# Second attention, second routing and second experts in one block, with the tokens, the first preparation and the position softmax laid out anew

## The chip, the cores and the metric

The kernel runs on one core of one Trainium2 chip. The metric is the device time of one execution in microseconds (us). The core has five engines that run their own instruction streams and meet at semaphores: PE (TensorE, matrix products), DVE (VectorE), ACT (ScalarE), POOL (GpSimd) and SP (SyncE, which here issues transfers). SBUF is the on-chip memory of 128 partitions, PSUM the eight banks into which PE writes.

## What is computed

The reference is an audio tower of two layers on 16 signals of 4096 samples. Cut to what matters:

```python
h = tok(x)          # cubic interpolation by 4, 255 windows of 64, 0.5*(x+1.3)^2 + 0.5*exp(-0.5*(x-0.7)^2),
                    # |FFT|, sigmoid mask against 0.12 of the row's maximum, soft minimum with 0.9 of it
h = h + attn0(layernorm(h))      # 8 heads, rank 32, values projected to 64 per head
h = h + ffn0(layernorm(h))       # 16 experts, top 2, relu, own layer norm behind it
h = h + attn1(layernorm(h))      # 8 heads of 8; (1-g)*softmax(q k) + g*softmax(position score)
h = h + moe(layernorm(h))        # 8 experts, top 2, gelu: out = tokens + sum_e combine_e * (h_e @ w2_e + b2_e)
```

A position score is `wpos0 * d + wpos2 * d*d + bias` with d the distance of two windows; its softmax over the windows doesn't depend on the signals. The 16 x 255 tokens of 64 numbers stand as 32 tiles of 128 x 64 (the last row of each second tile is padding).

## The kernel before, in words

The program is eight phases, one after the other, each a block of instruction streams with a barrier of all engines behind it (L161): `tokens`, `attention_prep0`, `attention0`, `experts0`, `attention_prep1`, `attention1`, `experts_prep1`, `experts1`. Inside a phase the order on each engine is written out by hand and the waits are semaphores; an engine that waits holds all that stands behind it in its stream. `link` (class `Chain`) makes an engine wait for its own last instruction.

*tokens.* SP and ACT issue the signal loads: 127 partitions of 16 runs of 20 samples from each queue (L222, L242), then single partitions, taps, constants and raw weights. `interpolate` (L209 to L216) multiplies and adds five taps; DVE does tile 0 (1024 elements a partition) and six batches of tile 1, POOL the other ten. ACT makes two squares and an exponential of each tile (L251 to L254), DVE sums them (L293) and splits the weights into three bf16 parts (L298 to L302); PE turns and transforms four groups (L361, L368), and ACT and DVE do the spectrum (L306 to L325). POOL then works out the position scores of eight heads (L345 to L347).

*attention_prep0.* Norm on DVE (L430 to L445), which writes each tile twice; PE turns it (L387), and `ColumnParts` splits the turned columns into three bf16 parts: ACT (L392, L398), DVE (L406, L408), POOL (L412).

*attention0.* 16 batches, two slots each. PE makes projections, scores (L636), turnings (L646) and outputs (L663); ACT the exponentials (L734), the copies of projections (L726) and of outputs (L742, once a batch). In the first four slots ACT also makes the exponentials of the position scores (L773) and DVE their maxima (`pos_max`, L848).

*experts0.* 8 chunks of 512 tokens, each 8 steps of two experts. PE: `hidden` (L1629), `second` (L1637), and for the next chunk columns (L1603), logits (L1611) and the turning of the combined weights (L1619). DVE: weighting (L1848), summing (L1828) and, as `extra` of each step, the routing of the next chunk (L1752 to L1785) and two norms. ACT: relu (L1720) and scalings. POOL: inverse roots (L531 to L540) and a copy a chunk (L1879). SP spreads the weights over partitions through DRAM (L1925).

*attention_prep1* makes values and position values and zeroes the padding on POOL.

*attention1.* 16 batches of four units (scores for the maximum, L1278 and L1431; turned scores, L1284; exponentials, L1399; outputs, L1294). A batch's tail (blend L1469, projection L1333, addition L1474, norm L518 to L543) runs up to three batches behind, so after the last unit there are eleven slots of tails alone.

*experts_prep1.* PE turns the tiles (L947) and multiplies by the router (L956); DVE takes the best two (L995 to L1002), and `combine` (L1013 to L1028) makes the weights of half the tiles at a time, in three bf16 parts; PE turns them (L964) and ACT copies them out (L977). POOL zeroes `ct` (L1042) and `selb`.

*experts1.* 8 chunks of two groups: PE `hidden` (L1070), `spread` of the weights (L1078), `second` (L1087) with three products for the output biases (L1091) and the turning of the sum (L1099); ACT gelu (L1138) and `y_out` (L1128); DVE weighting (L1169) and `finish` (L1157, L1158); SP stores each chunk with two transfers, of 128 and of 127 partitions (L1185). The lines of the biases are:

```python
for n in range(3):
    last = nc.tensor.matmul(Y[0:D], b2p[:, n], ct[:, c], start=False, stop=False)
```

## Time and profile before

| | us |
|---|---|
| median of 3 runs (909.3 to 911.83) | 911.78 |
| the profiled execution's own time | 908.39 |
| its span, first to last instruction | 906.5 |
| PE busy | 686.8 (76%) |
| DVE busy | 642.9 (71%) |
| ACT busy | 490.5 (54%) |
| POOL busy | 342.4 (38%) |

The phases end, by the timeline, near 98 (tokens), 126 (first preparation), 377 (first attention), 574 (first experts), 607 (second preparation), 805 (second attention), 840 (preparation of the second experts) and 906 us (second experts). A row of the timeline gives start, duration, engine, line, operation and tiles; "x4" means four merged into one row. PE's clock stands in the windows as a share of 2.4 GHz: 1.00, or 0.50 for 1.2 GHz.

### The profile page before, as it was taken

To read this page: it belongs to the slowest core of one execution; us is meant where nothing else is said; L and a number is where in the kernel's file an instruction comes from. 1 tells how busy PE (TensorE), PEld (TensorE's weight loads), DVE (VectorE), ACT (ScalarE), POOL (GpSimd) and SP (SyncE) were. 2 spreads that over 40 slices of the span, in tenths; PEclk is the share of its full clock that TensorE was granted. 3 is DMA by queue.
4 is the path that set the end of the run, shared out by engine and by line. 5 is a ranking of instruction groups with operands and counts; after the bars stand their busy time and mean duration, and the time that the engine had idled before them with its cause. 6 is when DMAs were issued, how large, how long until landed. Compare 5 with 4: busy or idle time off the path is not lost. (4 is left out here: it accounts for less than half of the span.)

```text
span 906.5 us, 16572 instructions
## 1 busy us (share of the span) xinstructions
PE 686.8 (76%) x5035; PEld 375.4 (41%) x5035; DVE 642.9 (71%) x1681; ACT 490.5 (54%) x1237; POOL 342.4 (38%) x374
## 2 busy tenths in 40 slices
PE   0003146899999999579999996568999999966995
PEld 0002124566666666323333322444555555556332
DVE  0299856988889889357788886746788888836343
ACT  0035446877677766245666664525666666622532
POOL 0299343577686776511122112442232222230000
PEclk9997557999999999889999998777999999965898
DMA  0200200000000000132323331000000000000000
GB/s 9 82 0 0 92 1 0 2 1 0 0 0 1 0 0 1 69 95 95 97 95 107 108 110 52 1 2 1 2 1 0 0 0 0 0 1 0 7 21 20
DMA packets 21241, 24.31 MB, mean 27 GB/s; under 512 B 11854, under 2 KB 12110, under 8 KB 20942
## 3 DMA queue, kind: packets, MB, share of 16 engines
q1 hardware_dynamic: 18989, 23.31, 8.3%
q10 hardware_dynamic: 2209, 0.49, 0.3%
q8 instruction: 19, 0.31, 0.1%
q14 instruction: 24, 0.20, 0.1%
HBM read 22.48 MB, written 1.31 MB: 26 GB/s over the span
## 5 line engine op out<-in xcount | busy, mean ns | idle before, releaser
L883 POOL TENSOR_TENSOR big<-big 128x1024 f32<-128x1024 f32 x64 | 120.4, 1893 | 80.7 <-DVE big L805 80.7
L734 ACT ACTIVATE big<-ps,big 128x255 f32<-128x255 f32 x256 | 117.5, 486 | 10.0 <-DVE big L799 9.5
L1720 ACT ACTIVATE big<-ps,b1s 128x512 f32<-128x512 f32 x128 | 80.5, 681 | 40.9 <-PE ps L1629 40.8
L799 DVE TENSOR_REDUCE big<-ps 128x4 f32<-128x1020 f32 x64 | 74.6, 1205 | 27.6 <-PE ps L636 27.6
L1431 DVE TENSOR_REDUCE big<-ps 128x4 f32<-128x1020 f32 x65 | 79.2, 1218 | 16.3 <-PE ps L1278 14.4
L812 DVE COPY mid<-ps 128x512 f32<-128x512 f32 x128 | 82.0, 681 | 5.7 <-DVE res L817 2.9
L1637 PE MATMUL ps<-big,w2s 128*64 128x512 f32 x256 | 69.0, 618 | 7.9 <-ACT big L1720 7.9
L1629 PE MATMUL ps<-big,wall 64*128 64x512 f32 x256 | 74.5, 650 | 0.0
L726 ACT ACTIVATE big<-ps 128x512 f32<-128x512 f32 x64 | 39.4, 616 | 64.0 <-PE ps L624 38.5
L646 PE MATMUL ps<-cst,big 128*128 128x128 f32 x512 | 71.1, 278 | 3.8 <-DVE mid L812 2.2
L1848 DVE SCALAR_TENSOR_TENSOR big<-ps,b2s,mid 128x512 f32<-128x512 f32 x64 | 48.0, 750 | 31.9 <-issue 12.0
L663 PE MATMUL ps<-mid,big 128*64 128x256 f32 (+1 forms) x512 | 69.5, 392 | 0.3 <-DVE mid L812 0.3
L1399 ACT ACTIVATE big<-ps 128x1024 f32<-128x1024 f32 x64 | 65.9, 1029 | 0.3
L646 PEld LDWEIGHTS ps<-cst,big 128*128 128x128 f32 x512 | 57.1, 141 | 20.8 <-DVE mid L812 7.8
L536 POOL TENSOR_TENSOR big<-big 128x4 f32<-128x4 f32 x16 | 16.1, 1009 | 120.6 <-DVE big L526 120.6
L1272 PE MATMUL ps<-big,selqk 128*128 128x256 bf16 x396 | 57.1, 283 | 3.5 <-POOL big L1509 2.4
L1369 ACT ACTIVATE big<-ps 128x256 bf16<-128x256 f32 x66 | 25.7, 389 | 61.4 <-PE ps L1272 61.3
L734 ACT ACTIVATION_READ_ACCUMULATOR big<-ps,big 128x1 f32 x256 | 56.3, 220 | 0.0
L361 PE MATMUL ps<-cst,big 128*128 128x128 f32 x16 | 3.6, 384 | 66.4 <-DVE big L293 66.4
L387 PE MATMUL ps<-cst,big 128*128 128x128 f32 x64 | 14.5, 373 | 49.7 <-DVE big L445 32.8
L636 PE MATMUL ps<-big 32*128 32x256 f32 x512 | 38.5, 417 | 8.2 <-ACT big L734 7.9
L1272 PEld LDWEIGHTS ps<-big,selqk 128*128 128x128 bf16 x396 | 34.3, 100 | 22.1 <-issue 13.9
(254 smaller groups left out, 1448.8 us busy)
## 6 DMA issues: line engine op xcount, KB each, us to landing
mid<-spread_w SPq DMA_DIRECT2D x128, 128.0 KB, 2.8
mid<-in_split_sel SPq DMA_DIRECT2D x1, 1536.0 KB, 6.2
wall<-in_w SPq DMA_DIRECT2D x1, 1280.0 KB, 7.1
cst<-in_consts SPq DMA_DIRECT2D x1, 666.5 KB, 5.0
mid<-in_w_raw SPq DMA_DIRECT2D x1, 620.0 KB, 6.3
w2s<-in_w SPq DMA_DIRECT2D x1, 512.0 KB, 3.2
out_tokens<-res SPq DMA_DIRECT2D x8, 64.0 KB
out_tokens<-res SPq DMA_DIRECT2D x8, 63.5 KB
```

Source lines behind the costliest of these rows:

```text
L646: last = nc.tensor.transpose(AT[:, j, c, P * tq:P * tq + P], e_sb[r % 4][:, j, tq, P * c:P * c + P], ident)
L663: last = nc.tensor.matmul(O[D * j:D * j + D, par], val[par][0:n, c, D * h:D * h + D], a_sb[r % 4][0:n, j, c], start=(g == 0 and a == 0 and ...
L734: last = nc.scalar.activation(e_sb[r % 4][:, jj, tq, 0:NW], S[:, 2 * (r % 2) + jj, tq, 0:NW], ACT.Exp, scale=-1.0, bias=minus[r % 4][:, jj ...
L799: nc.vector.tensor_reduce(minus[r % 4], S[:, 2 * a:2 * a + 2, :, 0:NW], AX.X, ALU.min).then_inc(s_mx, 1)
L812: nc.vector.tensor_copy(a_sb[r % 4][:, j], AT[:, j]).then_inc(s_at, 1)
L883: nc.gpsimd.tensor_tensor(e_sb[r % 4], e_sb[r % 4], bc(inverse[r % 4].unsqueeze(3), [P, 2, 2, 256]), ALU.mult).then_inc(s_A, 1)
L1272: last = nc.tensor.matmul(out_, selqk[:, 2 * p + n, part], parts[par][:, part], start=(part == 0), stop=(part == 2))
L1399: nc.scalar.activation(e_sb[(k - 1) % 4], T, ACT.Exp, scale=scale).then_inc(s_E, 1)
L1431: nc.vector.tensor_reduce(mx[k % 2], S[:, :, :, 0:NW], AX.X, ALU.max).then_inc(s_max, 1)
L1629: last = nc.tensor.matmul(H1(e, j), wst[0][half, f:f + P], xc[q][half], start=True, stop=True)
L1637: last = nc.tensor.matmul(Y(e)[D * j:D * j + D], w2s[0][:, 2 * e + j], hid[e % 2][j], start=True, stop=True)
L1720: last = nc.scalar.activation(hid[e % 2][j], H1(e, j), ACT.Relu, bias=b1s[0][:, 2 * e + j:2 * e + j + 1])
```

## The change

Seven parts:

1. The signal loads are cut into 112 and 15 partitions, and the taps go first on ACT's queue. DVE interpolates everything, in three stages (tile 0; two halves of tile 1), between which the weight splitting and the sums stand; ACT copies the weight parts; PSUM banks are no longer shared between groups. The absolute value moves from ACT to DVE, and products with broadcast maxima are joined with the sums.
2. The position scores leave `tokens` for POOL in `experts0`; maxima and exponentials leave `attention0` for DVE and ACT in `experts0`, one head a chunk.
3. `attention_prep0` splits the normed rows into bf16 parts before they are turned (`RowParts`), in place of the columns after.
4. The output biases of the second experts become one product of 96 rows: the combined weights are laid out three times (`c3`, with zeroed padding), the biases in three parts below each other.
5. `experts_prep1` and `experts1` move into the block of `attention1`. The turning, logits and routing stand between the tails of the last batches on PE, ACT and DVE.
6. `combine` and the turned weights come in two halves: `combine(1)` between the first and second chunk of the experts, the last four `weights` in chunk 2.
7. Each chunk is stored with four transfers, of 112 and 16 and of 112 and 15 partitions.

```diff
+                    sp.dma_start(sig[1:113, 0], windows(1, 112)).then_inc(s_sig[0], 16)
+                    sp.dma_start(sig[113:P, 0], windows(113, P - 113)).then_inc(s_sig[0], 16)
+                    sp.dma_start(sig[0:1, 0, :, 2:REACH], bass.AP(tensor=x.tensor, offset=0, ap=[[SIG, 1], [SIG, B], [1, REACH - 2]])).then_inc(s_sig[0], 16)
+                    sp.dma_start(raw, w_raw).then_inc(s_raw, 16)
+                    sp.dma_start(cst[:], consts).then_inc(s_cst, 16)
                     sp.dma_start(posw[:], pos_in).then_inc(s_pw_in, 16)
...
                     act.dma_start(tw, taps).then_inc(s_tw, 16)
+                    act.dma_start(sig[0:112, 1], windows(P, 112)).then_inc(s_sig[1], 16)
+                    act.dma_start(sig[112:P - 1, 1], windows(P + 112, P - 113)).then_inc(s_sig[1], 16)
+                    act.dma_start(sig[P - 1:P, 1], windows(NW - 1, 1)).then_inc(s_sig[1], 16)
...
+                    dve.wait_ge(s_sig[0], 16 * 3)
+                    dve.wait_ge(s_tw, 16)
                     link(nc.vector.tensor_copy(sig[0:1, 0, :, 0:2], bc(sig[0:1, 0, :, 2:3], [1, B, 2])))
-                    interpolate(nc.vector, link, 0, 0, B).then_inc(s_z[0], 1)
-                    interpolate(nc.vector, link, 1, B - 6, 6).then_inc(s_z2, 1)
-                    for t in (0, 1):
-                        dve.wait_ge(s_sq, 3 * t + 3)
-                        nc.vector.scalar_tensor_tensor(out=z[:, t].rearrange("p b j -> p (b j)"), in0=gauss[:, t].rearrange("p b j -> p (b j)"), scalar=0.5,
-                                                       in1=poly[:, t].rearrange("p b j -> p (b j)"), op0=ALU.mult, op1=ALU.add).then_inc(s_kw, 1)
-                    dve.wait_ge(s_raw, 16)
-                    hi, md, lo = (w64[:, s] for s in range(3))
-                    link(nc.vector.tensor_copy(hi, raw))
-                    link(nc.vector.tensor_tensor(raw_rest, raw, hi, ALU.subtract))
-                    link(nc.vector.tensor_copy(md, raw_rest))
+                    for k in (1, 2, 3, 4, 0):
+                        tap(*STAGES[0], k)
+                    dve.wait_ge(s_sig[1], 16 * 3)
+                    for k in (1, 2):
+                        tap(*STAGES[1], k)
+                    dve.wait_ge(s_hi, 1)
+                    nc.vector.tensor_tensor(raw_rest, raw, hi, ALU.subtract).then_inc(s_rest, 1)
+                    kernelled(0)
+                    for k in (3, 4, 0):
+                        tap(*STAGES[1], k)
...
-                    pool.wait_ge(s_sig, 16 * 4)
-                    interpolate(nc.gpsimd, link, 1, 0, B - 6).then_inc(s_z[1], 1)
...
+            def high(self, act, c, tiles):
+                nc.scalar.activation(self.ra[:, c, :, 0], tiles, ACT.Copy).then_inc(self.s_hi, 1)
+                nc.scalar.activation(self.rb[:, c, :, 0], tiles, ACT.Copy).then_inc(self.s_h2, 1)
+            def subtract(self, dve, c, tiles):
+                dve.wait_ge(self.s_hi, c + 1)
+                nc.vector.tensor_tensor(self.rest[:, c], tiles, self.ra[:, c, :, 0], ALU.subtract).then_inc(self.s_rest, 1)
+            def middle(self, act, c):
+                act.wait_ge(self.s_rest, c + 1)
+                nc.scalar.activation(self.ra[:, c, :, 1], self.rest[:, c], ACT.Copy).then_inc(self.s_md, 1)
+            def low(self, pool, c):
+                pool.wait_ge(self.s_md, c + 1)
+                nc.gpsimd.tensor_tensor(self.rb[:, c, :, 1], self.rest[:, c], self.ra[:, c, :, 1], ALU.subtract).then_inc(self.s_lo, 1)
+            def turn(self, pe, c):
+                pe.wait_ge(self.s_lo, c + 1)
+                pe.wait_ge(self.s_h2, c + 1)
+                if c >= self.RING:
+                    pe.wait_ge(self.s_col, 2 * (c - self.RING) + 2)
+                for k, rows in enumerate((self.ra, self.rb)):
+                    for t in range(TC):
+                        last = nc.tensor.transpose(self.turned[:, c % self.RING, k, P * t:P * t + P],
+                                                   rows[:, c, t].rearrange("p a d -> p (a d)"), ident_b[:])
+                last.then_inc(self.s_tr, 1)
+            def columns_out(self, dve, c):
+                dve.wait_ge(self.s_tr, c + 1)
+                for k in range(2):
+                    nc.vector.tensor_copy(columns[k][:, c], self.turned[:, c % self.RING, k]).then_inc(self.s_col, 1)
         def attention_prep0():
             sq = mid[:, 0:2048].rearrange("p (t d) -> p t d", t=NT)
...
+                    for c in range(CH + 3):
+                        if c < CH:
+                            normed(c)
+                        if 1 <= c <= CH:
+                            rows.subtract(dve, c - 1, xr[:, c - 1])
+                        if c >= 3:
+                            rows.columns_out(dve, c - 3)
...
-                        if known and j == 0:
-                            for h in (2 * k, 2 * k + 1):
-                                act.wait_ge(s_pmax, h + 1)
-                                for tq in range(2):
-                                    nc.scalar.activation(pexp[:, tq, h], pexp[:, tq, h], ACT.Exp, bias=pmax[:, tq, h:h + 1],
-                                                         accum_out=psum[:, tq, h:h + 1]).then_inc(s_pexp, 1)
...
+            c3 = mid[:, 3072:3072 + NT * 48].bitcast(BF16).rearrange("p (t r s) -> p t r s", t=NT, r=3)
...
+                    x_turn(0)
+                    x_turn(1)
+                    slot(B // 2, 2, ("tail",))
+                    logits(0)
+                    x_turn(2)
+                    slot(B // 2, 3, ("tail",))
+                    logits(1)
+                    x_turn(3)
+                    logits(2)
+                    x_turn(4)
+                    logits(3)
+                    x_turn(5)
+                    slot(B // 2, 6, ("tail",))
+                    logits(4)
+                    slot(B // 2, 7, ("tail",))
+                    x_turn(6)
+                    logits(5)
+                    x_turn(7)
+                    logits(6)
+                    logits(7)
+                    hidden(0, 0)
+                    pe.wait_ge(s_O, QUADS * B)
+                    pe.wait_ge(s_fin, B)
+                    for d in range(4):
+                        weights(d)
+                    for c in range(CH):
+                        hidden(c, 1)
+                        spread(c, 0)
+                        if c >= 1:
+                            second(c - 1, 1)
+                        if c == 2:
+                            pe.wait_ge(s_wgt, GROUPS * c + 1)
+                            for d in range(4, CH):
+                                weights(d)
+                        if c < CH - 1:
+                            hidden(c + 1, 0)
+                        spread(c, 1)
+                        if c >= 1:
+                            sum_turn(c - 1)
+                        second(c, 0)
+                    second(CH - 1, 1)
+                    sum_turn(CH - 1)
...
+                    columns_out(0)
+                    slot(B // 2, 2, ("o",))
+                    for c in range(1, 6):
+                        columns_out(c)
+                    slot(B // 2, 6, ())
+                    gap(0)
+                    for c in range(6, CH):
+                        columns_out(c)
+                    for d in range(4):
+                        weights(d)
+                    gap(1)
+                    for c in range(CH):
+                        for g in range(GROUPS):
+                            s = GROUPS * c + g
+                            act.wait_ge(s_h, s + 1)
+                            if s >= 2:
+                                act.wait_ge(s_wgt, s - 1)
+                            for n in range(2):
+                                last = nc.scalar.activation(hid[2 * g + n], H1(g, n), ACT.Gelu, bias=b1s[1][:, 2 * g + n:2 * g + n + 1])
+                            last.then_inc(s_hid, 1)
+                            if g == 0 and c >= 1:
+                                y_out(c - 1)
+                            if g == 0 and c == 2:
+                                for d in range(4, CH):
+                                    weights(d)
+                    y_out(CH - 1)
 
                 @block.vector
                 def _(dve):
...
+                        thrice = lambda a: bc(a[:, tl].unsqueeze(2), [P, half, 3, E])
+                        hi, md, lo = (c3[:, tl, :, E * n:E * n + E] for n in range(3))
+                        if n == 0:
+                            dve.wait_ge(s_pad3, 1)
+                        link(nc.vector.tensor_copy(hi, thrice(comb)))
+                        link(nc.vector.tensor_tensor(pick[:, tl], comb[:, tl], hi[:, :, 0], ALU.subtract))
+                        link(nc.vector.tensor_copy(md, thrice(pick)))
+                        nc.vector.tensor_tensor(lo, thrice(pick), md, ALU.subtract).then_inc(s_c3, 1)
...
+                    slot(B // 2, 1, ())
+                    best(0)
+                    slot(B // 2, 2, ())
+                    best(1)
+                    slot(B // 2, 3, ())
+                    best(2)
+                    slot(B // 2, 5, ())
+                    best(3)
+                    difference(0)
+                    slot(B // 2, 6, ())
+                    slot(B // 2, 7, ())
+                    slot(B // 2 + 1, 1, ())
+                    combine(0)
+                    slot(B // 2 + 1, 2, ())
+                    for c in range(4, CH):
+                        best(c)
+                    difference(1)
+                    for c in range(CH):
+                        weigh(c, 0)
+                        weigh(c, 1)
+                        if c == 0:
+                            combine(1)
+                        else:
+                            finish(c - 1)
+                    finish(CH - 1)
...
+                    nc.gpsimd.memset(c3, 0.0).then_inc(s_pad3, 1)
...
+                            for first, n in ((0, 112), (112, 16 - tq)):
+                                src = res[first:first + n].rearrange("p (b t) d -> p b t d", t=2)
+                                sp.dma_start(out[bass.ds(2 * c, 2), P * tq + first:P * tq + first + n].rearrange("b w d -> w b d"),
+                                             src[:, bass.ds(2 * c, 2), tq]).then_inc(s_out, 16)
...
-                            for n in range(3):
-                                last = nc.tensor.matmul(Y[0:D], b2p[:, n], ct[:, c], start=False, stop=False)
...
+                            last = nc.tensor.matmul(Y1[0:D], b2p[:], ct[0:96, c], start=False, stop=False)
...
+                        act.wait_ge(s_pmax, h + 1)
+                        for tq in range(2):
+                            nc.scalar.activation(pexp[:, tq, h], pexp[:, tq, h], ACT.Exp, bias=pmax[:, tq, h:h + 1],
+                                                 accum_out=psum[:, tq, h:h + 1]).then_inc(s_pexp, 1)
...
+                            if e == COLUMNS + 1:
+                                pos_exps(c)
...
+                    def pos_max(h):
+                        dve.wait_ge(s_pos, h + 1)
+                        link(nc.vector.tensor_reduce(pmax[:, :, h], pexp[:, :, h, 0:NW], AX.X, ALU.max))
+                        nc.vector.tensor_scalar(pmax[:, :, h], pmax[:, :, h], -1.0, None, ALU.mult).then_inc(s_pmax, 1)
...
-                        extra = [[first], [total, stats], [variance, second], [places], [shares, spread], [next_stats, next_variance], [gain, shift], [add]]
+                        extra = [[first], [total, stats], [variance, second], [places, lambda: pos_max(c)], [shares, spread], [next_stats, next_variance], [gain, shift], [add]]
...
+                    def pos_scores(h):
+                        link_p(nc.gpsimd.tensor_scalar(term, dist, posw[:, 0, h:h + 1], zb[:, h:h + 1], ALU.mult, ALU.add))
+                        link_p(nc.gpsimd.tensor_scalar(pexp[:, :, h], d2, posw[:, 2, h:h + 1], 0.0, ALU.mult, ALU.add))
+                        link_p(nc.gpsimd.tensor_tensor(pexp[:, :, h], pexp[:, :, h], term, ALU.add))
+                        nc.gpsimd.memset(pexp[:, :, h, NW:NW + 1], -1e30).then_inc(s_pos, 1)
...
+                        for h in ((0, 1), (2,), (3,), (4,), (5,), (6,), (7,), ())[c]:
+                            pos_scores(h)
...
-        phase(attention1)
-        phase(experts_prep1)
-        phase(experts1)
+        phase(attention1_and_experts1)
```

## Rows read from the trace of the kernel before

**Rows 1.** Windows of 50 us: stretch, length, busy time of each engine (instructions), PE clock, DMA share, GB/s.
```profile
450.00:500.00 50.00, 47.14 (x213) 15.55 (x211) 42.40 (x145) 33.88 (x65) 11.01 (x18) 1.00 0.31 98
```

**Rows 2.** Finer windows, same columns: the first load, and the last stores.
```profile
10.00:14.00 4.00, 0.00 (x0) 0.00 (x0) 0.00 (x0) 0.00 (x0) 0.00 (x0) 1.00 0.09 10
...
900.00:901.00 1.00, 0.00 (x0) 0.00 (x0) 0.00 (x0) 0.00 (x0) 0.00 (x0) 0.50 0.35 80
901.00:902.00 1.00, 0.00 (x0) 0.00 (x0) 0.00 (x0) 0.00 (x0) 0.00 (x0) 0.50 0.08 18
```

**Rows 3.** Timeline of the tokens: start us, us, engine, line, operation, out<-in, shape, [idle before].
```profile
1.15 30.85 SPq L225 DMA_DIRECT2D mid<-in_x  x1
...
40.10 1.23 DVE L209 TENSOR_TENSOR big<-mid 128x1024 f32<-128x1024 f32 x1 [4.27 <-DMA mid<-in_taps]
...
41.36 2.25 DVE L211 TENSOR_TENSOR mid<-mid 128x1024 f32<-128x1024 f32 x1
...
59.28 0.56 DVE L211 TENSOR_TENSOR mid<-mid 128x384 f32<-128x384 f32 x1
...
78.50 2.70 DVE L306 TENSOR_TENSOR big<-big 128x496 f32<-128x496 f32 x2
...
97.29 0.68 DVE L325 TENSOR_TENSOR res<-big 128x496 f32<-128x496 f32 x1
```

**Rows 4.** Timeline of the first preparation, and one row of the second attention.
```profile
110.36 0.69 DVE L406 TENSOR_TENSOR big<-ps,cols_area 64x512 f32<-64x512 f32 x1 [0.70 <-ACT cols_area L392]
...
124.68 1.15 POOL L412 TENSOR_TENSOR cols_area<-big,cols_area 64x512 bf16<-64x512 f32 x1 [0.34 <-ACT cols_area L398]
...
790.04 0.29 DVE L1453 TENSOR_TENSOR big<-big,ps 128x256 bf16<-128x256 bf16 x1
```

**Rows 5.** Timeline of ScalarE in the first attention: position exponentials, copies of the outputs.
```profile
152.37 0.56 ACT L773 ACTIVATE pexp<-pexp,pmax 128x256 f32<-128x256 f32 x1
...
152.86 0.55 ACT L773 ACTIVATE pexp<-pexp,pmax 128x256 f32<-128x256 f32 x1
...
166.68 0.39 ACT L742 ACTIVATE big<-ps 128x256 f32<-128x256 f32 x1
...
182.43 0.40 ACT L742 ACTIVATE big<-ps 128x256 f32<-128x256 f32 x1
...
196.47 0.39 ACT L742 ACTIVATE big<-ps 128x256 f32<-128x256 f32 x1
```

**Rows 6.** A maximum of positions; waits in the first experts: engine line <- for, us, times, longest.
```profile
127.77 0.67 DVE L848 TENSOR_REDUCE pmax<-pexp 128x2 f32<-128x510 f32 x1
...
PE ps L1637 <- ACT big L1720: 7.6, 8, 1.1
...
PE ps L1619 <- DVE big L1785: 2.1, 7, 0.9
```

**Rows 7.** Timeline of POOL: a zeroing of bf16.
```profile
805.91 3.51 POOL L1042 MEMSET big<- 128x4096 bf16 x1 [1.76 <-POOLq L161]
```

**Rows 8.** Timeline of the last three phases, and one logit product and one chain row.
```profile
795.74 1.07 PE L1294 MATMUL ps<-big,mid 128*32 128x256 f32 x16 [1.12 <-ACT big L1399]
...
804.19 0.60 DVE L543 TENSOR_SCALAR big<-res,big 128x128 f32<-128x128 f32 x2 [0.81 <-POOL big L531]
...
812.48 1.87 PE L956 MATMUL ps<-gates,big 64*128 64x8 f32 x8
...
829.74 0.62 DVE L1013 TENSOR_TENSOR big<-cst,big 128x128 f32<-128x128 f32 x2
...
845.08 1.28 DVE L1169 TENSOR_TENSOR big<-big,ps 128x512 f32<-128x512 f32 x2 [8.47 <-PE ps L1078]
...
898.21 0.43 DVE L1158 TENSOR_TENSOR res<-res,big 128x256 f32<-128x256 f32 x1
...
396.04 0.95 PE L1611 MATMUL ps<-gates,big 64*128 64x16 f32 x7
...
854.72 0.64 PE ps L1091 x3
```

680 lines of the change are left out of this document (310 added, 370 removed).

## Prediction

> **What bounds the kernel now.** I read the table of windows first, then the timeline of the stretches it made doubtful, then the waits. There is no one bound: the kernel is eight phases in a row, and each has its own. The first experts are held by TensorE (PE), 47.1 of 50 us busy at full clock, with VectorE (DVE) close behind at 42.4 [rows 1]. The start is held by a transfer: the small load of L225 sits 30.85 us in its queue, and the first interpolation operation starts at 40.10 us [rows 3]. Meanwhile the 16 DMA engines are 9% busy, about 1.5 of them, at 10 GB/s [rows 2]. Then DVE and GpSimd (POOL) take turns: a 128x1024 DVE operation takes 1.23 us when POOL comes second and 2.25 us right after; one of 384 elements with POOL out of the way takes 0.56 [rows 3]. The tokens end at 97.97 us. After the second attention comes a stretch in which nothing is full: the last normalised tile is written at 804.79, the first weighting of the second experts starts at 845.08 [rows 8]. From there PE is gapless.
>
> **Working, part by part.** The sum is made against the profiled execution: span 906.5 us, its own time 908.39; the median of the three runs is 911.78, so 3.4 above it.
>
> *Signal loads.* Each load of 127 partitions becomes one of 112 and one of 15, the taps go first on their queue and the constants come behind. The row shows two loads of 2032 pieces of 80 bytes at 10 GB/s: 325 KB in 31 us [rows 2]. A store of 128 rows beside one of 127 shows the other speed: 80 GB/s in its microsecond, against 18 GB/s for the 127-row one alone [rows 2]. That is some 240 pieces of 256 bytes in 1 us. At that pace 2032 pieces take about 8 us, at a sixteenth of the present time 2 us; with 2 us until the first byte moves and 1 to 2 us to land the first operation starts between 5 and 14 us. I take 8.5, nearer the low end, since that microsecond was not full. Gain 31.6, bounds 26 to 35. (The Trainium skill, DMA: Bandwidth & Descriptors, section on why a DMA increments its semaphore by 16, says that the number of engines is the largest k up to 16 that divides the outermost dimension: 127 gives 1, 112 gives 16, 15 gives 15. The 9% agrees; by it alone the operation would start at about 6.)
>
> *Interpolation on DVE alone.* Tile 0: seven operations of 1024 at 1.26 and two of 256 at about 0.45, 9.7 us. Tile 1 in two halves of 512: 5.7 each. Laid out with what stands between them on DVE (weight remainders 1.3 twice, sums of window parts 1.2 and 0.65), the last tap ends 25.7 us after the start. Then ScalarE (ACT) window parts 1.9, sum 0.6, and the last two groups through PE and ACT, 4.3: 32.5. The spectrum takes 19.5 us today from the power sums [rows 3], with POOL in the way; without it and with three fewer small operations I work out 14. Together 46.5, plus 1 for three POOL operations left in the stage: 47.5 against 57.9 today (40.10 to 97.97). Gain 10.4, bounds 7 to 13. (The Trainium skill, SBUF — State Buffer, section on two separate sides, calls this an exclusive lock, held for the whole instruction, between a DVE operation with two SBUF inputs and a POOL operation that reads SBUF; the alternation agrees.)
>
> *First preparation.* From the reciprocals on it takes 18 us today, to 125.83, at about 2.2 us of DVE a chunk (0.69 for the remainder [rows 4]). The new order is 0.42 + 0.42 and two copies of 512 bf16 out of PSUM. A bf16 addition out of PSUM of 256 takes 0.29 [rows 4], so 0.42 each, at worst 0.69. That is 1.7 to 2.2 us a chunk, with POOL's remainder in turns with it. Gain 1, bounds -3 to +3.
>
> *Position softmax.* It leaves POOL's part of the tokens (in the way, counted above) and ACT in the first attention: 16 exponentials, 0.49 us from one to the next [rows 5], 7.8 in all. The output copies stand 15.75 us apart with it and 14.04 after [rows 5], which is 0.85 a slot at least, four slots. Gain 5, bounds 3.4 to 7.8. It arrives in the first experts. There POOL's four instructions a head (about 2.5 us) have room. ACT's two exponentials fall where it has half a microsecond of slack and PE has none to lose before its next activation: about 0. DVE's maximum (0.67) and the negation behind it cost 0.90 a head [rows 6] and stand right ahead of the combining of weights. PE turns these weights and waits for them already today, 7 times, 2.1 us in all [rows 6]; it has no slack to give back. So 7 chunks by 0.9, 6.3. Turns with POOL in the same stretch: between 0 and 2 us a chunk, I take 0.4, as the maximum itself covers most of POOL's work. Loss 9, bounds 0 to 19.
>
> *Zeroing of the padded weights.* 3072 bf16 on POOL, ahead of the fetch for which the second attention's first projection waits; 4096 took 3.51 [rows 7]. Loss 2.6.
>
> *One block.* Its start is the end of the last full unit, 794.2. The first two turnings follow the last outputs at 796.8. With PE at work its clock stays at 2.4 GHz, where 7 small logit products take 0.95; at the present 1.2 GHz 8 take 1.87 [rows 8]. DVE then sets the pace: best(0) from 799.5, four routings of 1.3 with the remaining norms between them to 809.3, the last addition and its norm to 810.5, combine(0) 4.5 (3.45 for one today, and three of its operations grow threefold, 0.3 each) to 815, scale, four more routings to 821. Then weights out 2.4, a table load of 1.3 and the activation: first weighting at 826.3. PE idles 6 us before x_turn(7). If it falls to 1.2 GHz there and stays, 2 to 4 later; if the logits run at 1.2 GHz throughout, 832.8. Today 845.08: gain 18.8, bounds 12 to 20. The new waits on DVE hold back the last norms, behind them the last x_turn; that is in the sum.
>
> *Second experts.* 53.6 us from first weighting to last addition. Biases as one product: three take 0.64 in the chain [rows 8], so 0.43 a chunk, 3.4. Against it combine(1), 4.4 us on DVE where 2.05 were idle: 2.4; and the late weights in chunk 2, PE 1.5 and a late activation: 2.3. Net loss 1.3, bounds -1 to +4. Queue at the end: last addition at 898.64, span 906.5. The 127-row store runs until about 905 at 18 GB/s [rows 2]; now four issues and spread rows: gain 2.5, bounds 1 to 4.
>
> **Sum.** -31.6 - 10.4 - 1 - 5 + 9 + 2.6 - 18.8 + 1.3 - 2.5 = -56.4: 852.0 on the profiled execution's scale. The median of the runs stood 3.4 above the profiled execution and its lowest 0.9; I put 853.
>
> **Rivals.** (a) *The move into the first experts is hidden*: the stall of PE on its activations (7.6 us in 8 times [rows 6]) would absorb it. Against it: the weights are awaited behind that stall. Then 845. (b) *The move costs double*: POOL and DVE take turns for all of POOL's 2.5 us in the critical stretch, 0.9 + 1.8 by 7 chunks, 19 instead of 9: 863. For it: the 2.25 us row. Against: POOL begins while DVE reads PSUM. (c) *Small pieces are paced by how fast they are described, not by the engines*: at the 7.7 ns of today (31.3 us by 4064) 4064 pieces take 31 us in any split. With both halves in flight the first is done near 20 and the operation starts at 22: 867. Against it: the 80 GB/s row, less than 4 ns a piece. (d) *The routing in between pays little*: DVE waits at best(0) and best(1) while PE waits for DVE, clock at 1.2 GHz: first weighting past 835, 862. (e) *Slower*: DVE becomes the bound of the first experts because each of its two-input operations waits for POOL. It decides once a chunk grows from 21.05 to above 29.5 us (the 57 us and the 9 already counted, over 8 chunks); POOL's whole new work is 2.5 a chunk and ACT's 1, so it would have to be paid three times: 915. (f) *The loads do not spread at all*: start at 40 as now, 885.
>
> **Chances.** Forecast 0.55; (a) 0.16; (b) 0.11; (c) 0.07; (d) 0.07; (e) 0.01; (f) 0.03. The parts' own bounds, taken together, give about 10 either way; (a), (b) and (d) are inside 839 to 868 and (c) is at its edge, so this is the range. Measurements tell 0.3% apart, 2.7 us: faster 0.98, same 0.01, slower 0.01.
>
> **What would show it.** First interpolation operation at 6 to 10 us, and several DMA engines at once before it; 1024-element operations all near 1.25; tokens' end at 54 to 58. Output copies of the first attention 14.0 apart from the first on. Chunks of the first experts at 22.0 to 22.5 instead of 21.05, with PE waiting for the combined weights. First weighting of the second experts 32 us after the last full unit (today 51), chunks of 6.26 instead of 6.69, two of them longer. The prediction is wrong if the first operation starts past 15, if a chunk of the first experts passes 24, or if PE is at 1.2 GHz through the routing.

## The result, and the profile after the change

The changed kernel takes 870.63 us (median of 4 runs, 863.96 to 872.24) beside 911.45 for the kernel before (4 runs, 909.3 to 911.83): ratio 0.9548, 95% interval 0.9502 to 0.9595. The forecast was 853.0 with a range of 839 to 868. So the direction was right, and the gain is 41 us where 59 had been forecast. The profiled execution took 863.96 us with a span of 861.9. Against the forecast on the profiled scale, 852.0, that is 12 us too slow. The other 5.7 us lie between the profiled execution and the median: they are 6.7 us apart, where the forecast had put 1.0 (852.0 to 853). The profiled execution was the fastest of the four.

The page of the changed kernel, span, busy times and two of the slice rows:

```profile
span 861.9 us, 16537 instructions
...
PE 690.9 (80%) x5051; PEld 373.7 (43%) x5051; DVE 628.8 (73%) x1699; ACT 491.0 (57%) x1249; POOL 308.6 (36%) x372
...
PE   0404699999999983988889884566999999998897
...
PEclk9955599999999995999998998776999999995899
```

Look at the clock row, a slice of which is 21.5 us: the twenty-second (452 to 474 us) is an 8, in the middle of the first experts, which ran at full clock in all their chunks before the change. Slices this long hide the other, shorter falls.

The span falls apart into ten stretches. Each border is one instruction found in both timelines, and the forecast column is the prediction's own term:

| stretch, to | before | after | change | forecast |
|---|---|---|---|---|
| first interpolation operation starts | 40.10 | 6.98 | -33.1 | -31.6 |
| tokens' last operation ends | 57.87 | 48.94 | -8.9 | -10.4 |
| first attention's first fetch (POOL) | 28.71 | 26.41 | -2.3 | -1 |
| first experts' first fetch (POOL) | 252.6 | 247.3 | -5.3 | -5 |
| second preparation's first operation (POOL) | 195.2 | 214.8 | **+19.6** | +9 |
| second attention's first maximum (DVE) starts | 42.2 | 46.2 | +4.0 | +2.6 |
| its last maximum ends | 175.8 | 175.4 | -0.4 | 0 |
| second experts' first weighting starts | 52.5 | 35.9 | -16.7 | -18.8 |
| last addition ends | 53.6 | 55.7 | +2.1 | +1.3 |
| end of the span | 7.9 | 4.3 | -3.6 | -2.5 |
| sum | 906.5 | 861.9 | -44.6 | -56.4 |

Of the 11.8 us that are missing, 10.6 lie in the first experts. That is where the question was, and most experiments go there.

**The start** answers [rows 3]. DVE in the first microseconds of the changed kernel:

```profile
6.98 1.23 DVE L287 TENSOR_TENSOR big<-mid 128x1024 f32<-128x1024 f32 x1
8.24 1.23 DVE L289 TENSOR_TENSOR mid<-mid 128x1024 f32<-128x1024 f32 x1
```

The table of windows for the time of the loads (columns: stretch, its length, busy time of PE, PE's weight loads, DVE, ACT and POOL with counts, then the clock as a share of full speed, DMA share, GB/s), where [rows 2] had 10 GB/s:

```profile
2.00:6.00 4.00, 0.00 (x0) 0.00 (x0) 0.00 (x0) 1.20 (x1) 0.00 (x0) 1.00 1.15 196
```

The 196 GB/s are all that moved then, with taps, constants and weights. A share of 1.15 can't be taken as a share; beside the 0.09 of before it says that many DMA engines were at work.

**The first experts.** The waits of the stretch from the first weighting to the last turning of the weights. [Rows 6] had 2.1 us in 7 times here:

```profile
PE ps L1698 <- DVE big L1873: 12.7, 7, 1.8
```

PE now stands still 1.84 us in each of six chunks, and 1.64 us in the first, until DVE has added up the combined weights. One such chunk in the timeline (start, duration, and idle time of the engine before it in brackets; rows in between are left out):

```profile
423.71 0.88 DVE L1856 TENSOR_TENSOR big<-cst,big 128x64 f32<-128x64 f32 x2
423.71 0.80 POOL L1986 TENSOR_SCALAR mid<-cst,posw,small 128x512 f32<-128x512 f32 x1
424.62 0.69 DVE L1924 TENSOR_REDUCE pmax<-pexp 128x2 f32<-128x510 f32 x1
425.39 1.28 POOL L1988 TENSOR_TENSOR pexp<-pexp,mid 128x512 f32<-128x512 f32 x1
426.09 1.13 DVE L1916 TENSOR_TENSOR big<-big 128x512 f32<-128x512 f32 x1
428.38 0.22 DVE L1873 TENSOR_TENSOR big<-big 128x64 f32<-128x64 f32 x1
428.66 1.02 PE L1698 MATMUL ps<-cst,big 128*16 128x128 f32 x4 [1.85 <-DVE big L1873]
429.61 1.23 PE L1708 MATMUL ps<-big,wall 64*128 64x512 f32 x2
```

Two things stand ahead of the weights that did not before: the maximum (L1924), and POOL's score operations, beside which DVE's two comparisons take 0.88 instead of 0.49 and its addition 1.13 instead of 0.68. The last two rows show what the forecast had not thought of. The turning of the weights takes 1.02 us for four products where it takes 0.60 in an undisturbed chunk. The granted clock is in the table of windows, for the time ahead of the wait, right behind it and after that:

```profile
425.00:428.00 3.00, 1.08 (x4) 0.20 (x4) 2.83 (x8) 2.50 (x6) 1.68 (x3) 1.00 0.22 66
428.40:431.60 3.20, 2.94 (x8) 0.87 (x8) 2.62 (x13) 0.59 (x1) 0.32 (x1) 0.50 0.05 12
432.00:436.00 4.00, 4.00 (x20) 1.22 (x16) 3.14 (x5) 3.68 (x9) 1.31 (x4) 1.00 0.29 111
```

PE idles 1.85 us and then works at 1.2 GHz for over 3 us, with all of it on the path. A whole chunk without such a fall and the first with one:

```profile
368.00:390.80 22.80, 19.84 (x90) 6.65 (x90) 18.02 (x55) 13.58 (x28) 5.45 (x8) 1.00 0.25 86
413.50:437.50 24.00, 21.04 (x90) 6.78 (x89) 19.19 (x64) 14.94 (x32) 6.81 (x11) 0.93 0.28 94
```

The same 90 products take PE 1.2 us longer. In this execution it happens in four chunks, in one of them for 6.8 us instead of 3.4; chunks with a fall take 23.7 to 25.6 us from first weighting to first weighting, those without 22.7, apart from the first, 19.1 (before: 20.4 to 21.4, the first 18.1).

**The merged block** answers [rows 8]:

```profile
784.96 0.61 DVE L1486 TENSOR_TENSOR mid<-cst,mid 128x128 f32<-128x128 f32 x2
788.88 0.60 DVE L610 TENSOR_SCALAR big<-res,big 128x128 f32<-128x128 f32 x2
789.53 1.11 PE L1170 MATMUL ps<-cst,big 128*128 128x128 f32 x4 [3.10 <-DVE big L610]
790.58 3.37 PE L1184 MATMUL ps<-gates,big 64*128 64x8 f32 x15
796.00 1.94 PE L1190 MATMUL ps<-ident_b,mid 128*96 128x128 bf16 x16
799.29 1.28 ACT L1374 ACT_TABLE_LOAD   x1
801.94 0.69 DVE L1522 TENSOR_TENSOR big<-big,ps 128x512 f32<-128x512 f32 x1 [6.08 <-ACT big L1374]
```

The last scaling (L610) waits behind the combining of weights that begins at L1486; PE waits 3.10 us for it, and the turning of the finished weights (L1190), ready at 788.96, goes out at 796.00, behind logits at half speed. From 776.5 to 800 the clock is at 1.2 GHz:

```profile
776.50:800.00 23.50, 20.40 (x88) 15.76 (x88) 15.37 (x118) 5.54 (x13) 1.86 (x3) 0.50 0.00 1
```

### The profile page after: what moved, and what is told of

Its sections match the earlier page's. It is cut to its first block and busy times, and to the rows that moved or that the text cites. A ratio compares the mean times of both kernels' runs of the same rounds, so it can differ in the third digit from the quotient of the medians.

```text
span 861.9 us, 16537 instructions
## 1 busy us (share of the span) xinstructions
PE 690.9 (80%) x5051; PEld 373.7 (43%) x5051; DVE 628.8 (73%) x1699; ACT 491.0 (57%) x1249; POOL 308.6 (36%) x372
## 5 line engine op out<-in xcount | busy, mean ns | idle before, releaser
L1708 PE MATMUL ps<-big,wall 64*128 64x512 f32 x256 | 78.0, 678 | 0.0
L1716 PE MATMUL ps<-big,w2s 128*64 128x512 f32 x256 | 71.7, 640 | 7.6 <-ACT big L1806 7.6
L713 PE MATMUL ps<-cst,big 128*128 128x128 f32 x512 | 71.1, 278 | 3.5 <-DVE mid L872 1.8
L1071 PEld LDWEIGHTS ps<-big,selqk 128*128 128x128 bf16 x396 | 34.0, 99 | 22.0 <-issue 13.7
L1916 DVE TENSOR_TENSOR big<-big 128x512 f32<-128x512 f32 x56 | 41.9, 749 | 0.0
L1522 DVE TENSOR_TENSOR big<-big,ps 128x512 f32<-128x512 f32 x32 | 20.5, 683 | 28.7 <-ACT big L1374 18.2
```

The source lines that it names most:

```text
L713: last = nc.tensor.transpose(AT[:, j, c, P * tq:P * tq + P], e_sb[r % 4][:, j, tq, P * c:P * c + P], ident)
L1071: last = nc.tensor.matmul(out_, selqk[:, 2 * p + n, part], parts[par][:, part], start=(part == 0), stop=(part == 2))
L1708: last = nc.tensor.matmul(H1(e, j), wst[0][half, f:f + P], xc[q][half], start=True, stop=True)
L1716: last = nc.tensor.matmul(Y(e)[D * j:D * j + D], w2s[0][:, 2 * e + j], hid[e % 2][j], start=True, stop=True)
```

## The experiments

The theory: the first experts lose PE's wait for the combined weights, made of the maximum and of turns between DVE and POOL, and the clock that falls behind each wait; the rivals are in the expectations. The phase of the first experts is always read from its first fetch to the second preparation (195.2 before, 214.8 changed), and "the weightings' span" from the first to the last weighting (161.5 and 179.7). The median of the kernel before, run beside these, was 907.8 to 909.2 us.

**1. Whole loads.** `a_one_load`

```diff
-sp.dma_start(sig[1:113, 0], windows(1, 112)).then_inc(s_sig[0], 16)
-sp.dma_start(sig[113:P, 0], windows(113, P - 113)).then_inc(s_sig[0], 16)
+sp.dma_start(sig[1:P, 0], windows(1, P - 1)).then_inc(s_sig[0], 16)
```

(and the same on ScalarE's queue for the other half; DVE's waits are for two transfers a half instead of three)

> The changed kernel with each signal load whole again (127 partitions in one issue); the order of the queues (taps first, constants behind) stays as changed. Theory (the split decides): the first interpolation operation comes at 33 to 40 us instead of 6.98 and everything behind it moves by as much, so about 890 to 897 us for one execution that took 863.96. Rival 1 (the order of the queue did it, not the split): the first operation stays below 15 us and the time below 875. Rival 2 (each did a part): the first operation at 20 to 28 us.

901.87 us; span 899.0. DVE of this kernel:

```profile
37.50 1.22 DVE L285 TENSOR_TENSOR big<-mid 128x1024 f32<-128x1024 f32 x1
```

and a window of its load:

```profile
10.00:14.00 4.00, 0.00 (x0) 0.00 (x0) 0.00 (x0) 0.00 (x0) 0.00 (x0) 1.00 0.09 10
```

The rate is back at 10 GB/s and 9%. The split is worth 30.5 us (37.50 to 6.98), the order of the queues the other 2.6 (40.10 to 37.50). The time, one execution, rose by 37.9 and not by 31, past the 890 to 897 that were expected: the clock fell in six chunks instead of four, earlier in the routing and for longer behind the first weighting. The weightings' span is 182.6, the second experts 58.5 and the first weighting comes 37.5 us after the last maximum, 2.9, 2.8 and 1.6 more.

**2. Maximum behind the weights.** `b_max_late`

```diff
-[places, lambda: pos_max(c)], [shares, spread], [next_stats, next_variance],
+[places], [shares, spread], [next_stats, next_variance, lambda: pos_max(c)],
```

> The changed kernel with the position maximum of DVE moved behind the combining of the weights (from the fourth to the sixth place of a chunk of the first experts). The first experts, from their start to that of the next phase, take 214.7 us now and took 195.2 before. Theory A (the loss of 19.6 is PE's wait for combined weights, 0.9 a chunk from the maximum and about as much from turns with POOL, and a fall of PE's clock to 1.2 GHz that follows such a wait in the chunks from the fourth on): PE's wait for the last addition of the weights falls from 1.8 to about 0.9 us a chunk, the clock falls in fewer chunks, the phase takes 202 to 207 us. Rival B (turns with POOL alone are the loss): at most 2 us gained, 212 or more. Rival C (the clock falls for a reason apart from this wait): 208 to 209, the maximum's 6 us gained and all four falls still there.

865.88 us (864.94 to 868.21), ratio to before 0.9528 (0.9511 to 0.9545). The phase takes 212.8 us; PE's wait falls only from 1.84 to 1.55, and the clock fell in five chunks. That is rival B's number and misses theory A's. B's reading, that turns alone are the loss, does not hold all the same: experiment 3 takes them away and leaves 0.8 us a chunk. The timeline says why this edit gives so little:

```profile
425.91 1.72 POOL L1988 TENSOR_TENSOR pexp<-pexp,mid 128x512 f32<-128x512 f32 x1
426.53 1.12 DVE L1866 TENSOR_SCALAR big<-big 128x4 f32<-128x4 f32 x1
428.90 0.38 PE L1698 MATMUL ps<-cst,big 128*16 128x128 f32 x1 [1.56 <-DVE big L1873]
```

An operation of four elements (0.17 us elsewhere) takes 1.12 beside POOL's two-input addition and ends when that ends, at 427.6. In the changed kernel the maximum ran beside POOL's second multiplication (both 0.69), and what met POOL's addition first was DVE's weighting, which reads PSUM and took its usual 0.75. With the maximum gone from there, turns cost 1.55 - 0.21 = 1.3 us a chunk instead of the 0.8 that experiment 3 gives: the maximum had covered 0.5 us.

**3. Scores earlier on POOL.** `c_scores_early`

```diff
+for h in ((0, 1), (2,), (3,), (4,), (5,), (6,), (7,), ())[c]:
+    pos_scores(h)
 if c >= 1:
     own_root(c - 1)
-for h in ((0, 1), (2,), (3,), (4,), (5,), (6,), (7,), ())[c]:
-    pos_scores(h)
```

> The changed kernel with POOL's position scores of a chunk ahead of its wait for the variance instead of behind it, so that they no longer run beside the combining of the weights; the maximum of DVE stays where it is. Theory A: the comparison behind the combined weights is 0.48 again instead of 0.88 and the addition 0.68 instead of about 1.1, so 0.8 us less a chunk ahead of the weights, PE waits about 1.0 instead of 1.8, the clock falls in fewer chunks: the phase takes 203 to 208 us. Rival B (turns with POOL alone are the loss): 197 to 200, all of it gained. Rival D (the turns are only moved, to the weighting and additions of the chunk's ends): no gain, 212 or more.

858.62 us (853.81 to 861.3), ratio 0.9435 (0.9396 to 0.9475). The phase takes 205.5 us, PE's wait is 1.0 a chunk behind the first, and the clock fell in two chunks:

```profile
PE ps L1698 <- DVE big L1873: 7.7, 7, 1.6
```

Theory A's numbers. The turns are worth 1.84 - 1.0 = 0.84 a chunk; without them the maximum alone leaves 1.0 - 0.21 = 0.8.

**4. Both.** `d_both`

> Both edits together: maximum behind the combining of the weights, position scores ahead of POOL's wait. Theory A: nothing of the move is left ahead of the weights; PE waits for them 0.3 us a chunk as before the change, its clock never falls in the chunks, the phase takes 196 to 200 us, the kernel about 15 us less than the changed one, 855 us in the median, with less spread between runs. Rival C (the clock falls anyway): 202 to 206. Rival D (POOL and ACT hold the chunk wherever the work stands): 207 or more.

852.17 us (847.52 to 852.43), ratio 0.9352 (0.9323 to 0.938). The phase takes 199.5 us. Waits, and a chunk in the timeline:

```profile
PE ps L1698 <- DVE big L1873: 2.1, 7, 0.9
```

```profile
399.68 0.49 DVE L1856 TENSOR_TENSOR big<-cst,big 128x64 f32<-128x64 f32 x2
402.71 0.22 DVE L1873 TENSOR_TENSOR big<-big 128x64 f32<-128x64 f32 x1
402.99 0.60 PE L1698 MATMUL ps<-cst,big 128*16 128x128 f32 x4 [0.21 <-DVE big L1873]
405.37 0.68 DVE L1924 TENSOR_REDUCE pmax<-pexp 128x2 f32<-128x510 f32 x1
409.95 1.27 POOL L1988 TENSOR_TENSOR pexp<-pexp,mid 128x512 f32<-128x512 f32 x1
410.01 1.76 DVE L1916 TENSOR_TENSOR big<-big 128x512 f32<-128x512 f32 x1
```

The wait is what it was before the change, 2.1 us in 7 times, and the weightings ran at full clock throughout. The median is 3 us below the 855 that were expected. The turns have not gone: an addition at a chunk's end takes 1.76 instead of 0.68. There less waits for it, and a chunk is 21.6 us instead of 21.05. All the work of the move is still in this phase, at a cost of 199.5 - 195.2 = 4.3 us.

**5. The clock by itself.** `f_hold`, from the changed kernel, everything else in its old place

```diff
 pe.wait_ge(s_tot, c - 1)
+for n in range(3):
+    nc.tensor.matmul(R[:, 256:512], ident, cst[:, 0:256], start=True, stop=True)
 pe.wait_ge(s_comb, c + 1)
```

> The changed kernel with three products of 256 columns that nobody reads put on PE ahead of each chunk's wait for the combined weights (about 0.4 us each, in a wait of 1.84); nothing else is touched, the weights come as late as in the changed kernel. Theory A (the idle 1.84 us is what makes PE's clock fall; a fall costs 1.2 to 1.6 us of slower products on top of the wait): no stretch at 1.2 GHz in the chunks, the weightings of the first experts span 171 to 175 us instead of 179.7, the kernel 862 to 865 in the median. Rival C (the clock falls for a reason apart from this wait): falls as before, 179 to 185 us, since the products cost as well. Rival (the lateness of the weights is the whole cost, the clock follows without cost): within 1 us of 179.7 with no falls.

859.93 us (856.86 to 863.13), ratio 0.945 (0.9402 to 0.9498). The weights come as late as before the edit, 15.12 us after the chunk's start, but PE is at work meanwhile:

```profile
350.00:523.00 173.00, 161.24 (x705) 55.67 (x705) 140.61 (x452) 110.72 (x227) 43.66 (x68) 1.00 0.30 97
```

PE's wait is 0.35 us a chunk. No fall of the clock in the chunks, and the weightings' span is 173.0 instead of 179.7. So the idle time is what makes the clock fall, and the falls cost 6.8 us in the profiled execution. The lateness of the weights by itself is the rest of the span's growth, 173.0 - 161.5 = 11.5; 10.6 of it were PE's wait (12.7 - 2.1). The runs still lie 6.3 us apart, so the chunks are not the only place that makes them differ.

**6. The changed kernel again.** `m_after_again`

> The changed kernel once more, unedited, for its spread: its runs so far lie between 863.96 and 872.24 us, those of the kernel before within 2.5 us. Theory (the number of falls of PE's clock in the chunks of the first experts and at the start of the second experts differs from run to run, and each costs 1.2 to 1.6 us): the median is 866 to 872, and the phases before the first experts and the second attention repeat within 1 us of the first profile, all difference lying in the first experts and behind the last maximum. Rival (the spread comes from the loads or from the chip): a phase without falls of the clock moves by over 1 us.

868.06 us (864.99 to 873.27), ratio 0.9549 (0.9507 to 0.9591). The median lies where theory put it. This time the clock fell in six chunks, five of 24.2 to 24.3 us and one of 23.5, and for 10.2 us instead of 3.4 behind the first weighting. The weightings' span is 182.3 and the second experts take 58.5 us, 2.6 and 2.8 more than in the first profile. Each of the other stretches is within 1 us of it. A median 6.7 above the profiled execution fits this: more falls in the other runs than in the one that is shown. Chunk by chunk those others were not looked at.

**7. Zeroing beside the preparation** (on top of both edits). `g_zero_prep`

```diff
-nc.gpsimd.memset(c3, 0.0).then_inc(s_pad3, 1)          # second attention, ahead of fetch(0)
+link(nc.gpsimd.memset(mid[:, 3072:3072 + NT * 48].bitcast(BF16), 0.0))   # end of the preparation
```

> The version with both edits (852.17 us) and, besides, the zeroing of the padded weights on POOL at the end of the second preparation instead of at the start of the second attention. Theory (it stands alone in front of the first fetch where it is, and POOL is idle at the end of the preparation): from the first instruction of the preparation to the first maximum of the second attention 42.9 us instead of 45.6, the kernel 849.5. Rival (POOL becomes the end of the preparation, or the read of the residual there takes longer): 45 to 46, no gain.

From the preparation's start to the first maximum 42.6 us instead of 45.6, as expected. The kernel: 850.48 us (847.53 to 851.74), ratio 0.9362 (0.9324 to 0.94), which the times alone could not tell from 852.17; the phase does. In the changed kernel the row is

```profile
579.61 2.66 POOL L1594 MEMSET mid<- 128x3072 bf16 x1 [11.06 <-POOLq L161]
582.21 1.16 POOL L1559 COPY big<-cols_area 128x512 bf16<-128x512 bf16 x2
```

with POOL idle 11.06 us before it.

**8. Combining behind the last scaling** (on top of both edits). `h_combine_late`

```diff
-combine(0)
 slot(B // 2 + 1, 2, ())
+combine(0)
```

> The version with both edits and, besides, in the merged block the combining of the first half's weights (3.9 us of DVE) behind the last scaling of the residual instead of ahead of it. Theory (the last turning of x on PE waits for that scaling, and the turning of the weights stands behind it on PE, not behind the combining): the last turning of x comes 3 us earlier, the first weighting 34 to 35 us after the last maximum instead of 37.0, the kernel 849 to 850. Rival (DVE sets the pace; four routings now follow the combining and end when they ended before): within 0.5 us of 37.0. Rival (worse): the routings end 1 us later and the first weighting with them, 38.

847.93 us (844.89 to 851.54), ratio 0.9341 (0.9291 to 0.9391); the first weighting 31.0 us after the last maximum instead of 37.0.

```profile
769.25 0.60 DVE L610 TENSOR_SCALAR big<-res,big 128x128 f32<-128x128 f32 x2 [0.81 <-POOL big L598]
769.88 0.62 DVE L1486 TENSOR_TENSOR mid<-cst,mid 128x128 f32<-128x128 f32 x2
769.90 1.12 PE L1170 MATMUL ps<-cst,big 128*128 128x128 f32 x4 [0.85 <-DVE big L610]
776.37 1.94 PE L1190 MATMUL ps<-ident_b,mid 128*96 128x128 bf16 x16
```

PE's wait ahead of the last turning of x goes from 3.10 to 0.85. Not all 6 us are due to the edit: in this execution the clock stayed up until 13.5 us after the last maximum, in `d_both` until 9.0. The kernels with the old order show what that is worth: falls at 8.8, 10.2 and 11.6 us went with first weightings at 37.1, 36.0 and 34.9, so about 0.8 us for each microsecond. With the new order, falls at 8.4 and 8.7 us (the two kernels of 10) went with 34.5 and 34.2. At an equal fall the order is worth about 2.9 us, which is what the theory expected. This is read from kernels set side by side, and not from an edit of the clock.

**9. Keeping PE at work in the routing** (on top of both edits). `i_hold_routing`: fifteen products of 256 columns that nobody reads, in groups of one to six, between the turnings of x.

> The version with both edits and, besides, fifteen products of 256 columns that nobody reads, on PE between the turnings of x in the merged block, where PE waits for DVE. Theory (PE at 1.2 GHz through the routing, from 9 us after the last maximum for 24 us, is a cost that the forecast left out: it held PE at 2.4 GHz there): the clock stays at full speed to the first weighting or falls for less than 10 us, first weighting 33 to 35 us after the last maximum instead of 37.0, chunks of the second experts without the stretches at 1.2 GHz that follow (6.8 us of them today), last addition 89 to 91 us after the last maximum instead of 93.9. Rival (DVE sets the pace and the clock costs nothing): first weighting at 36.5 to 37.5. Rival (the products are in the way): 38 or more.

853.4 us (852.76 to 853.84), ratio 0.9387 (0.9352 to 0.9423), no better than the 852.17 without them; first weighting 39.4 us after the last maximum instead of 37.0. The clock fell 9.0 us after the last maximum all the same, ahead of the first of the products, and these then ran at half speed:

```profile
760.20:773.60 13.40, 13.40 (x46) 10.62 (x45) 6.19 (x53) 2.06 (x5) 1.16 (x2) 0.50 0.00 1
```

Without them the clock had stayed down for 24 us; here 13.7. What they gave back in clock they cost, and more, in PE's time. The third reading came true, and what the routing would take at full clock stays open.

**10. Four edits, and products in the second experts.** `k_gzh` has the edits of 2, 3, 7 and 8; `o_hold_second` adds

```diff
 spread(c, 0)
+if c == 0: hold(4)
 ...
+if c == 1: hold(4)
 spread(c, 1)
```

with hold(n) for n products of 256 columns into the bank of the turned sums.

> The changed kernel with four edits: maximum behind the combining of the weights, position scores ahead of POOL's wait, zeroing of the padded weights at the end of the second preparation, combining of the first half's weights behind the last scaling. Theory (the gains lie in different phases and add up): first experts 199.5, preparation to first maximum 42.7, first weighting of the second experts 31.0 after the last maximum, median 844 to 846 us. Rival (what the last two gain is given back to falls of the clock in the second experts): 848 or more.

> The version with four edits and, besides, four products of 256 columns that nobody reads after the first spreading of weights of the second experts, where PE waits 2.1 us for the first weighting, and four ahead of the spreading behind the combining of the second half's weights. Theory (the falls of the clock after the first weighting, 6.8 to 13.7 us long, come of these waits and are why the second experts take 56.5 to 59.3 us instead of the 53.6 before): 53.5 to 55.0 us from first weighting to last addition, runs within 2 us of each other, median 842 to 844. Rival (the clock falls at its own times and the products are in the way): 57 or more, no less spread.

`k_gzh`: 847.21 us (845.09 to 849.39), ratio 0.932 (0.9295 to 0.9345). First experts 199.4 and preparation to first maximum 42.8 as expected, but first weighting at 34.5 (the clock fell at 8.4) and second experts 58.4. So the median stands between theory's 846 and the rival's 848: the gains add up but for what earlier and longer falls take back. `o_hold_second`: **843.26 us** (841.03 to 845.49), ratio 0.927 (0.9244 to 0.9296), the fastest of all; second experts 55.7. The same stretch of 8 us behind the first weighting, of `k_gzh` and then of `o_hold_second`:

```profile
788.00:796.00 8.00, 8.00 (x28) 2.31 (x25) 4.65 (x11) 3.02 (x5) 0.00 (x0) 0.64 0.00 0
```

```profile
789.40:797.40 8.00, 8.00 (x39) 3.73 (x37) 5.16 (x11) 3.02 (x5) 0.00 (x0) 1.00 0.04 8
```

The clock stays up and PE gets through 39 products instead of 28. The gain, 2.8 us of the phase, is theory's; the phase ends 0.7 above the range that was expected, and the runs still spread over 4.5 us, not 2. In the last point the rival was right.

**11. Routing behind the attention** (from `k_gzh`). `n_routing_behind`: the four last steps of the attention on PE, their outputs on ScalarE and their slots on DVE all ahead of the first turning of x, the first columns out and best(0).

> The version with four edits, but the routing is taken from between the last steps of the second attention and put behind all of them, on PE, ScalarE and DVE; the merged block stays. Theory (the gain of the one block comes from the routing's running while the last samples are finished): first weighting 38 to 44 us after the last maximum instead of 31, the median 7 to 13 us above that of the version with four edits. Rival (the routing in between pays little, the gain is that of a phase's barrier and of the loads): 31 to 34, at most 3 us above.

853.31 us (849.93 to 854.74), ratio 0.9373 (0.934 to 0.9406), 6.1 us above `k_gzh`. First weighting 40.5 us after the last maximum instead of 34.5. So the interleaving is worth 6 us, and it does pay: the rival falls. In this is a clock that fell 5.0 us behind the last maximum instead of 8.4; how much of the 6 us that makes is not shown. The time rose a microsecond less than the least expected. If the interleaving is worth as much in the changed kernel, the other 10 us of the block's 16.7 lie in what else the merging changed (the barriers and the loads between the phases, the routing in two halves); these parts were not tried singly.

## Why the prediction was wrong

**Signal loads, hit.** Forecast 31.6, measured 33.1, first operation at 6.98 where 8.5 was put and 6 to 10 was the sign. The row that was trusted, 80 GB/s with 128 rows, named the mechanism but still undersold it: 196 GB/s in the window, with the other loads of that time. That the split does 30.5 us of it and the queue's order 2.6 is shown by experiment 1. Rivals (c) and (f) fall. (By the Trainium skill, DMA: Bandwidth & Descriptors, section on why a DMA increments its semaphore by 16, 127 rows go to one DMA engine and 112 to 16. The start that the prediction estimated from it alone, about 6, is nearer to the measured 6.98 than 8.5 is.)

**Interpolation, preparation, position exponentials: inside their bounds.** 8.9, 2.3 and 5.3 for 10.4, 1 and 5. The 1024-element operations take 1.23, the tokens end at 55.92, the output copies stand 14.0 us apart, the first two 13.75. These rest on the traces alone; no experiment undid them.

**Position softmax in the first experts: the step that failed.** "Loss 9, bounds 0 to 19"; measured 19.6. By its terms: the maximum and negation were put at 0.90 a chunk and the turns at 0.4, 1.3 together; the weights come 15.12 us after the chunk's start instead of 13.49, 1.63 a chunk. Scores moved away give 0.84 of that, the maximum the other 0.79. So the turns were sized at half. "The maximum itself covers most of POOL's work" is where that came from: it does cover some, but 0.5 us of the 1.3 that turns cost without it (experiment 2), and not most. With the clock at full speed the weightings' span grows by 11.5 us (experiment 5), of which 10.6 are PE's wait; 1.05 us more stand at the phase's head, where the first combining takes its turns with POOL, and 0.3 at its end. That is about 13 us where 9 were forecast.

The larger part of the miss, 6.8 us, was in no term. The prediction said that PE has no slack there and waits already, and priced a later arrival at the arrival's delay. It did not ask what PE's clock does in a wait nine times as long as the present one, although the same text reckoned with just that for the routing. Experiment 5 has it alone: with PE at work in the wait, 173.0 instead of 179.7. And all of it could be had for 4.3 us: where the maximum and the scores stood was the cost, not that they were there (experiment 4). Rival (b) was put at 19, with a chance of 0.11, for twice the turns. Its sum came true by luck and its reason did not; the measured turns are 0.84 a chunk against its 1.8. (The Trainium skill, SBUF — State Buffer, section on two separate sides, calls the pair of ports that DVE and POOL share an exclusive lock, which whichever starts first holds for its whole instruction. The four-element operation of experiment 2 agrees: it takes 1.12 us and ends with POOL's addition.)

The text named its own disproof: "if a chunk of the first experts passes 24, or if PE is at 1.2 GHz through the routing". Both came: chunks of 24.06, 25.56 and 24.28, and the clock down from 776.5 to 800. The phase passed its own upper bound of 19 by 0.6. The profiled execution alone, 863.96, would have lain between 839 and 868; the median of 870.63 did not.

**Zeroing, hit.** 2.6 forecast, 2.66 the row; the other 1.4 of that stretch goes with the preparation's clock, which came back 3 us later (27.2 us behind the preparation's start; before 24.3). In `a_one_load`, where it came back after 24.5, the stretch is 45.0, 2.8 above before. That it could stand elsewhere for nothing is shown by experiment 7.

**One block, a little short.** 16.7 for 18.8, first weighting 35.9 us behind the last maximum. "With PE at work its clock stays at 2.4 GHz" is false; it is rival (d)'s condition, but not rival (d)'s price: the first weighting came at 801.94, which with the earlier phases' 26.5 us added back is 828.4 and not past 835. By the kernels set side by side under experiment 8 (0.8 us for each microsecond that the clock falls earlier), the 2.1 us that are missing are what a fall 2.6 us later would give back; that is an estimate, since no run held the clock up through the routing. Experiment 8 shows that the routing was also held by an order the forecast had in its sum and did not question: the last scaling behind the combining.

**Second experts, short by an amount that differs from run to run.** 2.1 in the profiled execution for 1.3, 5 in the second profile. The chunks are 6.45 us apart and not 6.26, so the one product of the biases gains 0.24 a chunk and not 0.43: it takes 0.38 where 0.21 was reckoned. Over eight chunks that is 1.5 us, more than the 0.8 that are missing in the profiled execution. The 2.8 more of the second profile go with a clock that is down for 10.2 us instead of 3.4 behind the first weighting; experiment 10, in a kernel with the same long fall, takes 2.8 back.

**Profiled execution and median.** Put 1.0 apart; before the change they were 3.4 apart, and after it 6.7. With a clock that fell in four chunks of one profile of the changed kernel and in six of the other, that difference is the changed kernel's own.

**What stays open**: what the routing would take at full clock, the parts of the block's gain beyond the interleaving's 6 us, and why the clock falls behind some of the waits and not behind others.
